# Gates by tanh on ScalarE and two products on VectorE in place of silu, in a cross-attention and FP4 feed-forward kernel

## The chip, the cores and the metric

The kernel runs on one core of a Trainium2 chip. The metric is the device time in microseconds (us) of one execution. PE is TensorE, DVE is VectorE, ACT is ScalarE, POOL is GpSimd, SP is the queue that issues the DMAs.

## What is computed

Two layers, each with a residual, on x of 4096 rows (2 x 2048) by 512. The first is an additive cross-attention over 77 tokens, which takes a tanh of every (row, token, channel), reduces it over the 512 channels to scores `rho`, and makes of a softmax over the tokens two gates for each row. The second is a feed-forward layer whose inputs are quantised to FP4 in blocks of 16:

```
h = jnp.tanh(txt_proj[:, None, :, :] + feat_proj[:, :, None, :] + b)   # (rows, 77, 512)
rho = jnp.einsum('bftd,d->bft', h, w[:, 0])
att = jax.nn.softmax(rho + (1.0 - qm)[:, None, :] * NEG, axis=-1)
w_s, b_s = tanh(txt_h . Wcw + bcw), tanh(txt_h . Wcb + bcb)
x = x + w_s * layernorm(x) + b_s
...
gate = fp4_linear(x, w_gate)       # 512 -> 1408
y = fp4_linear(x, w_up)
h = jax.nn.silu(gate) * y
x = x + fp4_linear(h, w_down)      # 1408 -> 512
```

## The kernel before

The scores are made in four blocks of 1024 rows. A block has 77 "quads": ACT writes tanh for four (token, channel group) pairs by 1024 rows into a slot of a ring (`tanh_quad`, L619, four instructions), and PE multiplies the slot by `w` and adds it into the score bank `rho` (`score_quad`, L797). For some quads DVE adds the token's bias first (`sum_quads`, L966, four instructions), and ACT takes all four parts in one instruction (L614). The ring has two slots in block 1 and three in blocks 2 and 3, so ACT can start a quad only when PE is through with the one that had its slot.

The feed-forward layer runs over 32 tiles of 128 rows. A tile has four column groups n = 0 to 3 of 352. For each, PE fills a gate bank and an up bank (`gate_up`, L875; two pairs of banks, `gu0` for even and `gu1` for odd n), ACT makes silu of the gate bank in `sg` (`silu_gate`, L652), and DVE multiplies it by the up bank into `hbuf` (`hidden`, L1270), which frees the pair of banks for group n + 2. Then `quantise_hidden` (L986 to L1022) makes FP4 values of the tile's 1408 columns, a DMA turns them, and PE runs `down` (L889).

The layers overlap: while tiles 0 to 6 run, block 1 is scored, with tiles 7 to 14 block 2, with tiles 15 to 22 block 3. The order of each engine's work is written out: PE runs a `gate_up` or a third of a `down` and then one to three quads; ACT runs some quads ahead of PE and then a silu; DVE runs each group's `hidden`, the next tile's `rows_tile`, `quantise_hidden` and the sums. Nearly every DVE instruction waits for the one before it (`step`, `signal`).

At the end of a block (tiles 6, 14 and 22, `SOFTMAX_AT`) a softmax goes round the engines: DVE drains `rho` (L1185), PE turns it, DVE subtracts the maxima (L1193), ACT takes exp (L627), DVE sums (L1212 to L1218) into `garg`, ACT takes tanh of that (`softmax_gates`, L646), and DVE, for the last block POOL, makes the rows' factors from it. `FREE_FROM` is 22. From tile 23 on no quads are left, and ACT has little to do.

A function of ACT needs its set of tables. Where the set changes the compiler puts in an ACT_TABLE_LOAD.

Of the kernel before, what the change touches and what calls it, by code (L numbers as in the profile page):

```python
# [7 lines left out]
ALU = mybir.AluOpType  # L8
ACT = mybir.ActivationFunctionType
# [20 lines left out]
PART = 640  # L30


def bass_xattn_fp4_ffn(nc, x, ctx_in, mask_in, Ws_in, W_in, w_in, b_in, Wcw_in, bcw_in, Wcb_in, bcb_in,
# [3 lines left out]
    INNER = gate_in.shape[0]  # L37
# [5 lines left out]
    NT = BATCH * SEQ // P  # L43
# [5 lines left out]
    GU_N = INNER // 4  # L49
# [35 lines left out]
    for k in range(1, NBLK):  # L85
# [5 lines left out]
        n = QPB - (PRE_QUADS if k == 1 else 0)  # L91
# [9 lines left out]
    n = QPB + PRE_QUADS  # L101
# [25 lines left out]
    with ctx:  # L127
        def sb(name, shape, dt=F32):
            return ctx.enter_context(nc.sbuf_tensor(name, shape, dt))

        def pb(name, cols):
            return ctx.enter_context(nc.psum_tensor(name, [P, cols], F32))

        def sem(name):
            return ctx.enter_context(nc.semaphore(name))
# [22 lines left out]
        hbuf = work[:, 0:INNER]  # L158
# [3 lines left out]
        hq = hq_flat.rearrange("p (h d) -> p h d", h=2)  # L162
# [11 lines left out]
        sg = sb("sg", [P, 2, GU_N])  # L174
# [41 lines left out]
        h_ordered = spare[:, 5 * D:5 * D + INNER]  # L216
# [3 lines left out]
        last_hq = [last_room[:, 2 * a:2 * b] for a, b in PARTS]  # L220
        h_size = featT[:, 0, 0:INNER]
# [4 lines left out]
        gu = [[pb(f"gu{i}{n}", 512) for n in "gu"] for i in range(2)]  # L226
# [73 lines left out]
        sg_ready = sem("sg_ready")  # L300
        gu_drained = [sem(f"gu_drained{i}") for i in range(2)]
# [7 lines left out]
        h_ordered_ready = sem("h_ordered_ready")  # L309
# [240 lines left out]
        def _(act):  # L550
# [91 lines left out]
            def softmax_gates(k):  # L642
                act.wait_ge(garg_ready, k + 1)
                n = BLOCKS[k] // P
                for u in range(2):
                    act.activation(gates[:, u, 0:n], garg[:, u, 0:n], ACT.Tanh,  # L646
                                   bias=bc[:, u:u + 1]).then_inc(gates_ready, 1)

            def silu_gate(t, n):

                act.wait_ge(gu_filled[n % 2], 2 * t + n // 2 + 1)
                act.activation(sg[:, n % 2, :], gu[n % 2][0][:, 0:GU_N], ACT.Silu,  # L652
                               scale=1.0 / W_PRE).then_inc(sg_ready, 1)

            def rows_last(t):

# [16 lines left out]
            def order_hidden(t, a, b, count):  # L673

                act.wait_ge(gu_drained[0], 2 * t + (1 if b == PART else 2))
                act.wait_ge(gu_drained[1], 2 * t + (1 if b <= 3 * GU_N else 2))
                act.activation(h_ordered[:, a:b].rearrange("p (i q b) -> p i q b", q=QB, b=BPC),
                               hbuf[:, a:b].rearrange("p (i b q) -> p i q b", q=QB, b=BPC),
                               ACT.Copy).then_inc(h_ordered_ready, 1)
                act.wait_ge(h_ordered_ready, count)  # L680
# [10 lines left out]
            for t in range(NT):  # L691
                for n in range(GU_T):
                    while issued < min(before[t, n] + DEPTH[min(before[t, n], QUADS - 1) // QPB], QUADS):
                        tanh_quad(issued)
                        issued += 1
                    if t - 1 in SOFTMAX_AT and n == 0:
                        softmax_gates(SOFTMAX_AT[t - 1])
                    silu_gate(t, n)
                    if t == FREE_FROM and n == 2:
                        last_drain()  # L700
                    if t == NT - 1 and n == 1:
                        order_hidden(t, 0, PART, t - FREE_FROM + 1)
                if t in SOFTMAX_AT:
                    if issued < QUADS:
# [4 lines left out]
                    else:  # L709
                        softmax_exp(SOFTMAX_AT[t])  # L710
                if t == NT - 1:
# [9 lines left out]
        def _(pe):  # L721
# [182 lines left out]
            for t in range(NT):  # L904
                for p in range(7):
# [4 lines left out]
                    elif t > 0:  # L910
                        down(t - 1, p - 4)
                    if t in SOFTMAX_AT and p == 3 and t < FREE_FROM:
                        softmax_transposes(SOFTMAX_AT[t], 0)
                    for n in slots.get((t, p), ()):
# [14 lines left out]
        def _(dve):  # L929
            done, scales = [0], [0]  # L930

            def step(ins):

                done[0] += 1
                ins.then_inc(dve_step, 1)
                dve.wait_ge(dve_step, done[0])

            def signal(ins, s, count):

                ins.then_inc(s, 1)  # L940
                dve.wait_ge(s, count)
# [8 lines left out]
            tt = dve.tensor_tensor  # L950
            stt = dve.scalar_tensor_tensor
# [313 lines left out]

            def hidden(t, n, sums=True):

                dve.wait_ge(sg_ready, GU_T * t + n + 1)
                h = hbuf[:, n * GU_N:n * GU_N + GU_N]
                signal(tt(h, sg[:, n % 2, :], gu[n % 2][1][:, 0:GU_N], ALU.mult), gu_drained[n % 2], 2 * t + n // 2 + 1)  # L1270
                if sums:
                    sum_quads(before[t, n])

            def quantise_hidden(t, between=None, midway=None):
                lift = W_PRE
                if t > 0:
                    dve.wait_ge(h_turned, 16 * t)
                straight, size = None, hbuf
                if t >= FREE_FROM:
                    straight, size = (h_ordered[:, 0:INNER], h_ordered_ready, t - FREE_FROM + 1), h_size  # L1280
                signal(quantise(hbuf, INNER, hq[:, 0, :], hq[:, 1, :], size, SCALE_MIN * lift, H_PRE / lift,
                                straight=straight, at=before[t, 4], between=between,
                                midway=midway), hq_ready, t + 1)
                sum_quads(before[t, 5])

            def quantise_split(t, first, midway):

                dve.wait_ge(h_turned, 16 * t)
                a, b = slice(0, PART), slice(PART, INNER)
                step(quantise(hbuf[:, a], PART, hq[:, 0, a], hq[:, 1, a], hbuf[:, a], SCALE_MIN * W_PRE, H_PRE / W_PRE,  # L1290
                              midway=last_tops))
                hidden(t, 3)
                signal(quantise(hbuf[:, b], INNER - PART, hq[:, 0, b], hq[:, 1, b], h_size[:, b], SCALE_MIN * W_PRE,
                                H_PRE / W_PRE, straight=(h_ordered[:, b], h_ordered_ready, 1), first=first,
                                midway=midway), hq_ready, t + 1)

            def quantise_part(i):
                lift = W_PRE
                a, b = PARTS[i]
                n = b - a  # L1300
                signal(quantise(hbuf[:, a:b], n, last_hq[i][:, 0:n], last_hq[i][:, n:2 * n], hbuf[:, a:b], SCALE_MIN * lift,
                                H_PRE / lift, straight=(h_ordered[:, a:b], h_ordered_ready, NT - FREE_FROM + i)),
                       hq_ready, NT + i)

            def result(t):
# [12 lines left out]
            for t in range(NT):  # L1318
                begun = SOFTMAX_AT.get(t)
                ending = SOFTMAX_AT.get(t - 1)  # L1320
                if t not in (FREE_FROM + 1, FREE_FROM + 2):
                    hidden(t, 0)
# [67 lines left out]
```

## Time and profile before

| | |
|---|---|
| median of 3 runs | 1549.76 us (1546.88 to 1550.38) |
| the profiled execution | 1548.83 us |
| its span | 1547.0 us |
| busy: PE, ACT, DVE, POOL | 1436.5, 1363.7, 1179.6, 253.1 us |
| TensorE clock granted, mean | 0.983 |

The span is from the first to the last instruction of the core. An engine's busy time is a sum over stages with different limits, so it doesn't tell which engine sets the time of a stage. PE's instruction ends are modelled, and matmuls overlap, so their starts are what to read.

### The profile page before, as it was taken

To read this page: it belongs to the slowest core of one execution; us is meant where nothing else is said; L and a number is where in the kernel's file an instruction comes from. 1 tells how busy PE (TensorE), PEld (TensorE's weight loads), DVE (VectorE), ACT (ScalarE), POOL (GpSimd) and SP (SyncE) were. 2 spreads that over 40 slices of the span, in tenths; PEclk is the share of its full clock that TensorE was granted. 3 is DMA by queue.
4 is the path that set the end of the run, shared out by engine and by line. 5 is a ranking of instruction groups with operands and counts; after the bars stand their busy time and mean duration, and the time that the engine had idled before them with its cause. 6 is when DMAs were issued, how large, how long until landed. Compare 5 with 4: busy or idle time off the path is not lost.

```text
span 1547.0 us, 24416 instructions
## 1 busy us (share of the span) xinstructions
PE 1436.5 (93%) x9752; PEld 648.6 (42%) x9752; DVE 1179.6 (76%) x1956; ACT 1363.7 (88%) x1269; POOL 253.1 (16%) x433
## 2 busy tenths in 40 slices
PE   6979899866989999999999999989999999999998
PEld 3434444411333333333444444434444444555554
DVE  6499999864486666759676766698877787898887
ACT  5999999999999999999999999999999999433321
POOL 1032222210011011101011111011111111312211
PEclk9999999988999999999999999999999999999999
DMA  4133333330011111102111111112111111123332
GB/s 145 41 72 82 82 83 82 82 68 29 12 26 40 27 40 40 34 16 45 40 40 40 40 27 40 40 30 50 40 40 40 40 40 40 40 59 73 79 69 61
DMA packets 181878, 77.91 MB, mean 50 GB/s; under 512 B 163947, under 2 KB 165995, under 8 KB 181765
## 3 DMA queue, kind: packets, MB, share of 16 engines
q1 hardware_dynamic: 180544, 75.00, 21.3%
q8 instruction: 76, 1.25, 0.3%
q10 hardware_dynamic: 1221, 1.36, 0.3%
q14 instruction: 37, 0.30, 0.1%
HBM read 27.85 MB, written 8.39 MB: 23 GB/s over the span
## 4 chain that ended last, share of the span: by engine, by line
PE 51%; ACT 23%; DVE 22%; issue 2%; DMA 1%; POOL 1%; SPq 0%; ACTq 0%; DVEq 0%; POOLq 0%
PE rho L797 19%; ACT hring L619 14%; PE dn L889 10%; PE gu0g L875 5%; PE gu1g L875 5%; PE gu1u L875 5%; PE gu0u L875 5%; ACT hring L614 4%; DVE work L1000 2%; DVE work L1018 2%; DVE work L1019 2%; DVE featT L966 2%; DVE sm L986 2%; ACT featT L614 1%; ACT featT L619 1%
## 5 line engine op out<-in xcount | busy, mean ns | idle before, releaser
L619 ACT ACTIVATE hring<-featT,bias 128x1024 f32<-128x1024 f32 x708 | 751.1, 1160 | 10.2 <-PE rho L797 10.2
L797 PE MATMUL rho<-hring,wslide 128*32 128x512 f32 x3776 | 461.2, 614 | 56.8 <-ACT hring L619 49.5
L619 ACT ACTIVATE featT<-featT,bias 128x1024 f32<-128x1024 f32 x232 | 249.5, 1182 | 1.2 <-PE rho L797 1.2
L797 PEld LDWEIGHTS rho<-hring,wslide 128*32 128x32 f32 x3776 | 106.2, 111 | 333.7 <-issue 197.6
L889 PE MATMUL dn<-wd_room,turned 128*128 128x512 f16 x1023 | 230.6, 379 | 0.4 <-DMA turned<-work 0.3
L485 POOL TENSOR_SCALAR split_t<-sm 128x88 f32<-128x88 f32 (+3 forms) x93 | 22.7, 245 | 1138.7 <-DVE sm L989 1138.6
L614 ACT ACTIVATE hring<-featT 128x4096 f32<-128x4096 f32 x57 | 208.1, 3651 | 0.6 <-DVE featT L966 0.6
L966 DVE TENSOR_SCALAR featT<-featT,bias 128x1024 f32<-128x1024 f32 x256 | 175.5, 750 | 10.0 <-ACT hring L614 6.3
L1270 DVE TENSOR_TENSOR work<-sg,gu1u 128x352 f32<-128x352 f32 x64 | 33.4, 521 | 166.6 <-ACT sg L652 165.7
L889 PEld LDWEIGHTS dn<-wd_room,turned 128*128 128x128 f16 x1023 | 96.5, 98 | 145.4 <-issue 36.0
L797 PE MATMUL rho<-featT,wslide 128*32 128x512 f32 x1056 | 126.3, 596 | 4.0 <-ACT featT L619 3.2
L875 PE MATMUL gu1g<-wg,turned 128*128 128x352 f16 x768 | 125.4, 313 | 4.3 <-DVE work L1270 4.3
L875 PE MATMUL gu0g<-wg,turned 128*128 128x352 f16 x768 | 125.5, 313 | 4.0 <-DVE work L1270 3.2
L875 PE MATMUL gu1u<-wu,turned 128*128 128x352 f16 x768 | 125.0, 313 | 0.0
L875 PE MATMUL gu0u<-wu,turned 128*128 128x352 f16 x768 | 125.0, 313 | 0.0
L488 POOL TENSOR_TENSOR s_lo<-sm,s_hi 128x88 f16<-128x88 f32 (+3 forms) x93 | 110.3, 1186 | 7.3
L875 PEld LDWEIGHTS gu0g<-wg,turned 128*128 128x128 f16 x768 | 71.3, 98 | 75.4 <-issue 27.7
L875 PEld LDWEIGHTS gu1g<-wg,turned 128*128 128x128 f16 x768 | 71.8, 98 | 72.7 <-issue 28.5
L875 PEld LDWEIGHTS gu0u<-wu,turned 128*128 128x128 f16 x768 | 75.1, 98 | 39.4
L875 PEld LDWEIGHTS gu1u<-wu,turned 128*128 128x128 f16 x768 | 75.2, 98 | 39.3
L652 ACT ACTIVATE sg<-gu1g 128x352 f32<-128x352 f32 x64 | 30.8, 481 | 60.6 <-PE gu1u L875 60.6
L652 ACT ACTIVATE sg<-gu0g 128x352 f32<-128x352 f32 x64 | 30.9, 483 | 52.9 <-PE gu0u L875 52.8
(207 smaller groups left out, 1573.3 us busy)
## 6 DMA issues: line engine op xcount, KB each, us to landing
xt<-in_x SPq DMA_DIRECT2D x32, 256.0 KB, 2.9
out<-xt SPq DMA_DIRECT2D x32, 256.0 KB, 2.3
work<-in_x SPq DMA_DIRECT2D x10, 512.0 KB, 3.9
xt<-in_x SPq DMA_DIRECT2D x6, 512.0 KB, 3.9
xt<-in_L_ffn_w_gate SPq DMA_DIRECT2D x11, 256.0 KB, 2.8
xt<-in_L_ffn_w_up SPq DMA_DIRECT2D x11, 256.0 KB, 2.7
work<-in_L_ffn_w_down SPq DMA_DIRECT2D x2, 704.0 KB, 4.4
xt<-in_L_ffn_w_down SPq DMA_DIRECT2D x2, 704.0 KB, 4.3
```

The source lines that it names most:

```text
L488: pool.tensor_tensor(s_lo[:, 0:nb], s, s_hi[:, 0:nb], ALU.subtract).then_inc(split_ready, 1)
L614: act.activation(slot[s], featT[:, :, r:r + rows], ACT.Tanh).then_inc(tanh_ready, GRP)
L619: act.activation(slot[s][:, g, :], featT[:, e, ROW0[k]:ROW0[k] + rows], ACT.Tanh, bias=bias[:, e, base + tok:base + tok + 1]).then_inc(tan ...
L652: act.activation(sg[:, n % 2, :], gu[n % 2][0][:, 0:GU_N], ACT.Silu, scale=1.0 / W_PRE).then_inc(sg_ready, 1)
L797: last = pe.matmul(rho[SLOTW * g:SLOTW * g + SLOTW, hf * 512:hf * 512 + 512], wslide[:, e, SLOTW - 1 - r:2 * SLOTW - 1 - r], slot[s][:, g, ...
L875: last = pe.matmul(ps[:, 0:GU_N], xqT[:, a, k, :], w[:, bb, k, n * GU_N:n * GU_N + GU_N], start=(k == 0 and i == 0), stop=(k == KC - 1 and ...
L889: last = pe.matmul(dn[:, :], hqT[:, a, c, :], wd[:, bb, c, :], start=(c == 0 and i == 0), stop=(c == NC - 1 and i == 2))
L966: dve.tensor_scalar(featT[:, g, to:to + BLOCKS[k]], featT[:, e, ROW0[k]:ROW0[k] + BLOCKS[k]], bias[:, e, tok:tok + 1], None, ALU.add).then ...
L986: step(dve.tensor_reduce(am, v, axis=AX_X, op=ALU.max, apply_absolute_value=True))
L1000: ins = tt(a.rearrange("p (i q b) -> p i b q", **natural), src.rearrange("p (i b q) -> p i b q", **natural), r.rearrange("p (i b) -> p i b ...
L1018: step(tt(a, a, m, ALU.add))
L1270: signal(tt(h, sg[:, n % 2, :], gu[n % 2][1][:, 0:GU_N], ALU.mult), gu_drained[n % 2], 2 * t + n // 2 + 1)
```

## The change

For tiles before `BY_TANH` = `FREE_FROM` + 1 = 23, the gate is no longer silu(g) times u. ACT makes tanh(g / 2), DVE makes (tanh + 1) times g in one scalar_tensor_tensor that reads the gate bank, and then multiplies by u. The result is silu(g) times u, up to a constant factor that `lift` takes out in the quantisation. From tile 23 on silu stays. Tanh and exp lie in one set of tables, silu and tanh in another one in common.

```
@@ constants
+    BY_TANH = FREE_FROM + 1
+
+    def lift(t):
+        return 2.0 * W_PRE * W_PRE if t < BY_TANH else W_PRE
@@ silu_gate
                 act.wait_ge(gu_filled[n % 2], 2 * t + n // 2 + 1)
-                act.activation(sg[:, n % 2, :], gu[n % 2][0][:, 0:GU_N], ACT.Silu,
-                               scale=1.0 / W_PRE).then_inc(sg_ready, 1)
+                if t < BY_TANH:
+                    act.activation(sg[:, n % 2, :], gu[n % 2][0][:, 0:GU_N], ACT.Tanh,
+                                   scale=0.5 / W_PRE).then_inc(sg_ready, 1)
+                else:
+                    act.activation(sg[:, n % 2, :], gu[n % 2][0][:, 0:GU_N], ACT.Silu,
+                                   scale=1.0 / W_PRE).then_inc(sg_ready, 1)
@@ hidden
                 dve.wait_ge(sg_ready, GU_T * t + n + 1)
-                h = hbuf[:, n * GU_N:n * GU_N + GU_N]
-                signal(tt(h, sg[:, n % 2, :], gu[n % 2][1][:, 0:GU_N], ALU.mult), gu_drained[n % 2], 2 * t + n // 2 + 1)
+                if t < BY_TANH:
+                    step(stt(h, sg[:, n % 2, :], 1.0, gu[n % 2][0][:, 0:GU_N], ALU.add, ALU.mult))
+                    signal(tt(h, h, gu[n % 2][1][:, 0:GU_N], ALU.mult), gu_drained[n % 2], 2 * t + n // 2 + 1)
+                else:
+                    signal(tt(h, sg[:, n % 2, :], gu[n % 2][1][:, 0:GU_N], ALU.mult), gu_drained[n % 2], 2 * t + n // 2 + 1)
@@ the quantisers of hbuf: W_PRE becomes lift(t) in two constants, no instruction changes
```

ACT's order at the end of block 2 (tile 14 and the first group of tile 15), before. `stage` is the softmax's room, `gates` its result, `sg` the gate of a group; `hring` and `featT` are slots of the ring.

```order
L619 ACTIVATE hring<-featT,bias 128x1024 x4
L627 ACT_TABLE_LOAD
L627 ACTIVATE stage<-stage 128x4x77 x2
L619 ACTIVATE featT<-featT,bias 128x1024 x4
L614 ACTIVATE hring<-featT 128x4096
L619 ACTIVATE hring<-featT,bias 128x1024 x4
L646 ACTIVATE gates<-garg,bc 128x8 x2
L652 ACT_TABLE_LOAD
L652 ACTIVATE sg<-gu0g 128x352
```

The same place of the changed kernel, whose lines are numbered four or five higher there:

```order
L623 ACTIVATE hring<-featT,bias 128x1024 x4
L631 ACTIVATE stage<-stage 128x4x77 x2
L623 ACTIVATE featT<-featT,bias 128x1024 x4
L618 ACTIVATE hring<-featT 128x4096
L623 ACTIVATE hring<-featT,bias 128x1024 x4
L650 ACTIVATE gates<-garg,bc 128x8 x2
L657 ACTIVATE sg<-gu0g 128x352
```

Two table loads are gone here, and nothing changes places. Over the whole program there were eight loads, ahead of the first copy, the first silu, each block's exp from block 1 on and the first silu after it; two stand in the changed kernel, the first and the one ahead of tile 23's silu.

DVE's order at the drain of block 2's scores (tile 14), before; `work` holds `hbuf`:

```order
L1185 TENSOR_SCALAR stage<-rho,negm 128x1024
L1270 TENSOR_TENSOR work<-sg,gu0u 128x352
L966 TENSOR_SCALAR featT<-featT,bias 128x1024 x4
L1192 TENSOR_REDUCE mx<-tr 128x4
L1193 TENSOR_TENSOR stage<-tr,mx 128x4x77
L1192 TENSOR_REDUCE mx<-tr 128x4
```

and in the changed kernel:

```order
L1193 TENSOR_SCALAR stage<-rho,negm 128x1024
L1279 SCALAR_TENSOR_TENSOR work<-sg,gu0g 128x352
L1280 TENSOR_TENSOR work<-work,gu0u 128x352
L974 TENSOR_SCALAR featT<-featT,bias 128x1024 x4
L1200 TENSOR_REDUCE mx<-tr 128x4
L1201 TENSOR_TENSOR stage<-tr,mx 128x4x77
L1200 TENSOR_REDUCE mx<-tr 128x4
```

One instruction more stands ahead of each product with the up bank, 92 in all (23 tiles of four groups), and everything behind it on DVE keeps its place.

## Rows read from the trace of the kernel before

**Rows 1.** Busy time by stage: start:end, length, busy us (instructions) of each engine.
```profile
core 0: us, PE busy (x) PEld busy (x) DVE busy (x) ACT busy (x) POOL busy (x), PEclk, DMA share, GB/s
395.00:693.00 298.00, 275.40 (x1983) 109.59 (x1982) 203.69 (x286) 296.05 (x249) 35.42 (x52) 1.00 0.14 29
693.00:1002.00 309.00, 303.13 (x2189) 127.67 (x2187) 223.67 (x323) 308.92 (x281) 42.64 (x60) 1.00 0.18 40
1002.00:1079.00 77.00, 71.65 (x511) 31.48 (x508) 71.58 (x122) 75.15 (x68) 11.10 (x16) 1.00 0.23 40
1080.00:1290.00 210.00, 209.99 (x1524) 89.80 (x1523) 161.00 (x225) 210.00 (x178) 29.77 (x44) 1.00 0.17 38
```

**Rows 2.** Groups of ACT's table loads: count, busy us, mean ns, idle before.
```profile
L652 ACT ACT_TABLE_LOAD x4 | 5.1, 1283 | 0.1
...
L627 ACT ACT_TABLE_LOAD x2 | 2.6, 1283 | 0.0
```

**Rows 3.** Timeline of ACT at 385 to 397: start, length, instructions merged.
```profile
384.72 10.49 ACT L619 ACTIVATE hring<-featT,bias 128x1024 f32<-128x1024 f32 x10
...
396.52 0.46 ACT L652 ACTIVATE sg<-gu0g 128x352 f32<-128x352 f32 x1
```

**Rows 4.** Groups of DVE's instructions, shapes kept apart.
```profile
L1270 DVE TENSOR_TENSOR work<-sg,gu1u 128x352 f32<-128x352 f32 x64 | 33.4, 521 | 166.6 <-ACT sg L652 165.7
...
L1309 DVE SCALAR_TENSOR_TENSOR xt<-dn,xt 128x512 f32<-128x512 f32 x31 | 21.4, 690 | 0.8
```

**Rows 5.** Timeline of DVE at 418 to 448, idle before and its releaser in brackets.
```profile
418.26 0.52 DVE L1270 TENSOR_TENSOR work<-sg,gu1u 128x352 f32<-128x352 f32 x1 [5.77 <-ACT sg L652]
...
437.05 0.52 DVE L1270 TENSOR_TENSOR work<-sg,gu0u 128x352 f32<-128x352 f32 x1
437.60 0.52 DVE L1270 TENSOR_TENSOR work<-sg,gu1u 128x352 f32<-128x352 f32 x1
...
445.29 2.74 DVE L966 TENSOR_SCALAR featT<-featT,bias 128x1024 f32<-128x1024 f32 x4
```

**Rows 6.** Timeline of ACT at 448.
```profile
448.14 3.62 ACT L614 ACTIVATE hring<-featT 128x4096 f32<-128x4096 f32 x1 [0.57 <-DVE featT L966]
```

**Rows 7.** Timeline of DVE at 678 to 719.
```profile
678.39 1.28 DVE L1185 TENSOR_SCALAR stage<-rho,negm 128x1024 f32<-128x1024 f32 x1 [9.16 <-PE rho L797]
...
718.84 0.52 DVE L1270 TENSOR_TENSOR work<-sg,gu1u 128x352 f32<-128x352 f32 x1 [0.30 <-ACT sg L652]
```

**Rows 8.** Timeline of PE at 720: tile 7's last gate.
```profile
719.73 1.95 PE L875 MATMUL gu1g<-wg,turned 128*128 128x352 f16 x12
```

**Rows 9.** Timeline of DVE at 1002 to 1085.
```profile
1002.45 1.28 DVE L1185 TENSOR_SCALAR stage<-rho,negm 128x1024 f32<-128x1024 f32 x1 [8.95 <-PE rho L797]
...
1040.86 0.52 DVE L1270 TENSOR_TENSOR work<-sg,gu0u 128x352 f32<-128x352 f32 x1
...
1078.30 0.52 DVE L1270 TENSOR_TENSOR work<-sg,gu0u 128x352 f32<-128x352 f32 x1
...
1084.93 0.52 DVE L1270 TENSOR_TENSOR work<-sg,gu1u 128x352 f32<-128x352 f32 x1 [6.11 <-ACT sg L652]
```

**Rows 10.** Timeline of PE at 1079: tile 16's third gate.
```profile
1078.87 1.96 PE L875 MATMUL gu0g<-wg,turned 128*128 128x352 f16 x12 [0.29 <-DVE work L1270]
```

**Rows 11.** Timeline of ACT at 1033: the gates of block 2.
```profile
1032.87 0.49 ACT L646 ACTIVATE gates<-garg,bc 128x8 f32<-128x8 f32 x2 [0.94 <-DVE garg L1218]
```

**Rows 12.** Timeline of DVE at 1273.
```profile
1273.10 0.51 DVE L1270 TENSOR_TENSOR work<-sg,gu0u 128x352 f32<-128x352 f32 x1
```

**Rows 13.** Timeline of PE at 1274 and 1311.
```profile
1274.35 1.95 PE L875 MATMUL gu0g<-wg,turned 128*128 128x352 f16 x12
...
1310.89 1.92 PE L797 MATMUL rho<-hring,wslide 128*32 128x512 f32 x16
```

**Rows 14.** Timeline of ACT at 1313: its last two quads.
```profile
1313.46 4.40 ACT L619 ACTIVATE hring<-featT,bias 128x1024 f32<-128x1024 f32 x4
```

**Rows 15.** Timeline of DVE at 1322 to 1332: tile 22's last two groups.
```profile
1322.47 0.52 DVE L1270 TENSOR_TENSOR work<-sg,gu0u 128x352 f32<-128x352 f32 x1 [0.80 <-ACT sg L652]
...
1331.37 0.52 DVE L1270 TENSOR_TENSOR work<-sg,gu1u 128x352 f32<-128x352 f32 x1
```

More of the change, by code:

```diff
@@ L1266, in hidden @@
             def hidden(t, n, sums=True):
+                h = hbuf[:, n * GU_N:n * GU_N + GU_N]
                 dve.wait_ge(sg_ready, GU_T * t + n + 1)
-                h = hbuf[:, n * GU_N:n * GU_N + GU_N]
-                signal(tt(h, sg[:, n % 2, :], gu[n % 2][1][:, 0:GU_N], ALU.mult), gu_drained[n % 2], 2 * t + n // 2 + 1)
+                if t < BY_TANH:
[3 more added lines that the diff above has]
+                    signal(tt(h, sg[:, n % 2, :], gu[n % 2][1][:, 0:GU_N], ALU.mult), gu_drained[n % 2], 2 * t + n // 2 + 1)
                 if sums:
@@ L1280, in quantise_hidden @@
                     straight, size = (h_ordered[:, 0:INNER], h_ordered_ready, t - FREE_FROM + 1), h_size
-                signal(quantise(hbuf, INNER, hq[:, 0, :], hq[:, 1, :], size, SCALE_MIN * lift, H_PRE / lift,
+                signal(quantise(hbuf, INNER, hq[:, 0, :], hq[:, 1, :], size, SCALE_MIN * lift(t), H_PRE / lift(t),
                                 straight=straight, at=before[t, 4], between=between,
@@ L1289, in quantise_split @@
                 a, b = slice(0, PART), slice(PART, INNER)
-                step(quantise(hbuf[:, a], PART, hq[:, 0, a], hq[:, 1, a], hbuf[:, a], SCALE_MIN * W_PRE, H_PRE / W_PRE,
+                step(quantise(hbuf[:, a], PART, hq[:, 0, a], hq[:, 1, a], hbuf[:, a], SCALE_MIN * lift(t), H_PRE / lift(t),
                               midway=last_tops))
                 hidden(t, 3)
-                signal(quantise(hbuf[:, b], INNER - PART, hq[:, 0, b], hq[:, 1, b], h_size[:, b], SCALE_MIN * W_PRE,
-                                H_PRE / W_PRE, straight=(h_ordered[:, b], h_ordered_ready, 1), first=first,
+                signal(quantise(hbuf[:, b], INNER - PART, hq[:, 0, b], hq[:, 1, b], h_size[:, b], SCALE_MIN * lift(t),
+                                H_PRE / lift(t), straight=(h_ordered[:, b], h_ordered_ready, 1), first=first,
                                 midway=midway), hq_ready, t + 1)
             def quantise_part(i):
-                lift = W_PRE
                 a, b = PARTS[i]
                 n = b - a
-                signal(quantise(hbuf[:, a:b], n, last_hq[i][:, 0:n], last_hq[i][:, n:2 * n], hbuf[:, a:b], SCALE_MIN * lift,
-                                H_PRE / lift, straight=(h_ordered[:, a:b], h_ordered_ready, NT - FREE_FROM + i)),
+                signal(quantise(hbuf[:, a:b], n, last_hq[i][:, 0:n], last_hq[i][:, n:2 * n], hbuf[:, a:b], SCALE_MIN * lift(NT - 1),
+                                H_PRE / lift(NT - 1), straight=(h_ordered[:, a:b], h_ordered_ready, NT - FREE_FROM + i)),
                        hq_ready, NT + i)
```

1 line of the change is left out of this document (removed).

## The prediction

> **What bounds the kernel now.** I read the stages first [rows 1]. From 395 to 1290 ACT is busy nearly all the time, 296.1 of 298 us, 308.9 of 309, 75.2 of 77 and 210.0 of 210, so at first sight whatever leaves ACT shortens the kernel. PE has idle time in the first stage (22.6 us) and the second (5.9), but none in the fourth: 209.99 of 210. There both engines are full, and a delay of PE that enters it comes out at its end. In the third stage, around the softmax of block 2, DVE is the busy one: 71.6 of 77 us.
>
> Then I went down DVE's timeline and looked for where it waits, since the change gives work to it. Over the whole run it waits some 167 us for the silus of odd groups alone [rows 4], but not everywhere. From 1002.45, where it drains the scores that PE has just ended, to 1084.93, where it waits for ACT again, there is no idle time on it but a wait for PE's transposes, which themselves wait for DVE [rows 9]. At the end of that run PE stands and waits for DVE's product: gate group 2 of tile 16 can start at 1078.87 only because the product that began at 1078.30 has ended [rows 9, 10]. The same shape stands at the end of block 1: DVE runs from 678.39 to 718.84 with 0.30 us of idle time that ACT ended, and the product that starts then ends at 719.36, 0.37 before PE's last gate of tile 7 needs its bank [rows 7, 8].
>
> **What the change removes.** By the two orders six loads go, not five: the first silu's, two each at the ends of blocks 1 and 2, and the last exp's. Each lasted 1.28 us [rows 2]. What a load costs its queue is read from starts: ten tanhs begin at 384.72 and last 10.49, so, at 1.04 from start to start, the next instruction would begin at 395.12; behind the load it begins at 396.52 [rows 3]. That is 1.40 a load. Five lie where ACT is full: 7.0 us. The sixth, at tile 22, is worth nothing, since DVE is busy with that tile's quantisation and has the exps before it asks for them.
>
> The Trainium skill ("ScalarE: Activation LUTs", What ACT_TABLE_LOAD costs) gives 2.66 us for a switch, 1.28 for the load and 1.38 for a drain. By it five loads would be 13.3 us. The trace shows the 1.28 and no drain behind it, and the sum goes by the 1.40.
>
> **What it adds.** Tanh in place of silu on the same 352 columns costs ACT the same, by the nearest rows: both are one pass at about one column a ns. DVE gets 92 scalar_tensor_tensors, half of whose operands lie in PSUM. The product beside it is of the same size, with one operand in PSUM: 0.52 [rows 4]; two such follow each other at 0.55 [rows 5]. The instruction of that very form in the trace is 512 wide and takes 0.69 [rows 4]. So a piece costs between 0.55 and 0.72 from start to start; I take 0.555, as the width is 352. In all 51 us, most of it under DVE's waits for ACT. What counts is how many stand in each run of DVE that has no idle time and whose end somebody waits for:
>
> (A) Block 1. DVE waits for ACT at 418.26; from there three pieces (tile 0 group 3, tile 1 groups 0 and 1) come before the sum that starts at 445.29 and ends 2.74 later, and ACT has already waited 0.57 us for it [rows 5, 6]. 3 x 0.555 = 1.7 us later, against 1.4 gained just before: ACT goes on at +0.3, the sign being that of a loss. Other sums of this block are in time by 0.6 or more behind a single piece, as I read them one by one, and cost nothing.
>
> (B) End of block 1, counted from PE's last score. Four pieces (tile 6 groups 2 and 3, tile 7 groups 0 and 1) stand between the drain and the end of the product at 718.84: 2.2, less the 0.30 of idle time and the 0.37 in hand, so PE's gate of group 3 starts 1.6 later [rows 7, 8]. ACT meanwhile has two loads less, 2.8, of which it waits away 0.9 for the softmax's sums. But a ring of three slots ties it to a PE that is 1.6 late, and most of its lead goes. PE has the stage's 5.9 us of idle time, nearly all waits for ACT, to win back what it lost [rows 1]. I put both at +0.2 when block 2's last score is done. With (A): +0.5.
>
> (C) End of block 2. Seven pieces stand in the run from 1002.45 to the end of the product at 1078.30: tile 14 groups 2 and 3, the four of tile 15, tile 16 group 0 [rows 9]. 7 x 0.555 = 3.9 us, and PE waits for its end already [rows 10]. The two loads that ACT loses here don't help: it waits for the softmax's sums as it is, 0.94 us [rows 11], which come 1.1 later now, and the products are held by DVE and not by silus. So PE enters the full stage at +4.4; I write +4.3 for what of ACT's gain DVE may use.
>
> (D) To the end of block 3. PE can't win it back [rows 1]. Around 1273 four pieces since DVE's last wait (2.2 us) meet 0.73 us in hand [rows 12, 13], by which PE falls back another 1.3 against ACT. ACT's second last quad starts at 1313.46, and the slot is that of the quad which PE ends about 1312.8, 1.9 after it started at 1310.89 [rows 13, 14]: 0.6 in hand. So ACT is dragged behind PE to +4.8.
>
> (E) Tile 22. ACT's last silu frees the product at 1322.47, behind 0.80 us of idle time that takes up what DVE is late by but 0.3; from there to the gates of the last softmax DVE runs without a stop, with that product and the one at 1331.37 on its way [rows 15]: 0.3 + 2 x 0.555 = +1.4.
>
> Behind tile 23 nothing is changed. Sum: 0.3 + 0.2 + 3.8 + 0.5 + 1.4 = +6.2 us. The profiled execution took 1548.83, 1.8 more than its span, and would take 1555.0; the median of the runs shown is 0.9 above it. I say 1555.5. About 0.2% (3 us) is what a measurement of this kernel can tell from no change.
>
> **The rivals.** (1) ACT's gain comes through, faster. This needs DVE's runs to have more room than I read: the gates at (C) would have to be released by ACT and not by DVE. Then 7.0 is gained, 1.4 is lost at (E), and the time is 1549.8 - 5.6 = 1544. The decision falls at 1078.87: from 3.9 us in hand there it holds, and the row shows a wait of 0.29 instead [rows 10]. For it speaks only that ACT is full in every stage [rows 1]. By the page's 2.66 a load the gain would be 6.3 us more, and the time 1538; what speaks against it is the row. Chance 0.13 for both.
>
> (2) Losses and gains nearly cancel: (A) and (C) are as written, but ACT keeps the 1.9 it leads by at (B), PE follows it over the stage's idle time, and 1 to 2 us of (D) and (E) stay hidden. That gives +1 to +3, about 1551.5. Chance 0.22.
>
> (3) The piece costs more than the product beside it, up to 0.72, being of a form with three operands that reads a bank beside that which PE fills. All costs, 3, 4, 7, 4 and 2 pieces, grow by 0.165 each, some 3.3 us, and the time is about 1559. Chance 0.10.
>
> My forecast, +6.2 by DVE's full runs, has 0.55.
>
> **How the numbers follow.** Slower by over 0.2% are my forecast and (3), 0.65 together. Of (2) most lies within 0.2%: 0.22. Faster is (1): 0.13. The range leaves out (1) and the top of (3): it starts at 1547.5, the low side of (2) less the spread of runs, and ends at 1559.5. The likeliest case alone: 1553 to 1558.
>
> **What would show it.** Two table loads on ACT; a busy time of DVE higher by 48 us and of ACT lower by 7.7. ACT waiting about 2 us for the sum at tile 1. PE's wait for a product at tile 16, now 0.29, grown to 2 us or more, and the tile 7 one new. ACT waiting for PE's quads in blocks 2 and 3, where it waits for almost nothing now; its wait for `garg` at tile 15 at 3 us. From tile 23 on the stretch to the end as long as before. The prediction is wrong if PE's gates at tiles 7 and 16 start no later behind the block's last score than before, or if the fourth stage has idle time on PE that takes up the delay.

## The result and the profile after

The changed kernel takes 1556.49 us, the median of 6 runs (1555.02 to 1559.39), against 1549.22 us before in 6 runs. The ratio is 1.0044, with a 95% interval of 1.0034 to 1.0054: slower by 5.3 to 8.4 us. The profiled execution spans 1553.2 us, 6.2 more than the one before.

The sums of the page move as the orders say. This is the busy line of the changed kernel; DVE has 47.4 us more, for 92 instructions more, and ACT 7.4 less. PE's share is unchanged.

```profile
PE 1439.0 (93%) x9752; PEld 650.4 (42%) x9752; DVE 1227.0 (79%) x2048; ACT 1356.3 (87%) x1263; POOL 252.3 (16%) x433
```

The groups of the changed kernel (line, engine, operation, count, busy us, mean ns, idle before) give the prices. The added operation takes 521 ns, like the product beside it, so the piece is 0.555 and not 0.72. Of eight loads two are left. A gate by tanh takes 453 ns.

```profile
L1279 DVE SCALAR_TENSOR_TENSOR work<-sg,gu1g 128x352 f32<-128x352 f32 x46 | 23.9, 521 | 129.8 <-ACT sg L657 129.2
L563 ACT ACT_TABLE_LOAD x1 | 1.3, 1283 | 2.4 <-issue 2.4
L660 ACT ACT_TABLE_LOAD x1 | 1.3, 1283 | 0.0
L657 ACT ACTIVATE sg<-gu1g 128x352 f32<-128x352 f32 x46 | 20.8, 453 | 4.3 <-PE gu1u L883 4.3
```

Now the places of the prediction, one after the other. DVE's timeline of the changed kernel at the end of block 2, which answers to [rows 9]:

```profile
1003.40 1.28 DVE L1193 TENSOR_SCALAR stage<-rho,negm 128x1024 f32<-128x1024 f32 x1 [8.13 <-PE rho L805]
...
1082.58 0.51 DVE L1279 SCALAR_TENSOR_TENSOR work<-sg,gu0g 128x352 f32<-128x352 f32 x1
1083.13 0.52 DVE L1280 TENSOR_TENSOR work<-work,gu0u 128x352 f32<-128x352 f32 x1
...
1087.63 0.52 DVE L1279 SCALAR_TENSOR_TENSOR work<-sg,gu1g 128x352 f32<-128x352 f32 x1 [3.98 <-ACT sg L657]
```

And PE's, at tile 7's last gate, tile 16's third and tile 21's third, which answer to [rows 8, 10, 13]:

```profile
722.07 1.96 PE L883 MATMUL gu1g<-wg,turned 128*128 128x352 f16 x12 [1.19 <-DVE work L1280]
...
1083.71 1.96 PE L883 MATMUL gu0g<-wg,turned 128*128 128x352 f16 x12 [1.66 <-DVE work L1280]
...
1280.44 1.96 PE L883 MATMUL gu0g<-wg,turned 128*128 128x352 f16 x12 [1.10 <-DVE work L1280]
```

From the drain to the product that PE waits for DVE has no idle time but its wait for the transposes, as before. From the drain's start to the start of tile 16's third gate it was 1078.87 - 1002.45 = 76.42 us, and it is 1083.71 - 1003.40 = 80.31 now: 3.89 more, seven pieces of 0.555. The three gates start 2.3, 4.8 and 6.1 us later than before, each behind a wait for DVE that has grown or is new; at tile 16 it is 1.66 us, where the prediction named 2 or more.

Stages of the changed kernel (start:end, length, busy us of PE, PEld, DVE, ACT, POOL; granted clock), the fourth moved with the work:

```profile
1003.00:1084.00 81.00, 74.96 (x512) 32.69 (x509) 75.22 (x129) 74.64 (x68) 11.13 (x16) 0.96 0.19 38
1084.00:1297.00 213.00, 211.90 (x1535) 90.71 (x1533) 173.91 (x249) 211.18 (x179) 29.84 (x44) 1.00 0.19 38
```

The fourth stage has 1.1 us of idle time on PE, which is its wait at 1280 and no room to win anything back.

One thing stands there that wasn't forecast: a granted clock of 0.96 in the third stage, where before it was 1.00. Four stretches of 3.4 us at the lower of TensorE's two levels, 1.2 GHz, come up at 437, 686, 1011 and 1045, where the kernel before has none between 386 and its end.

### The profile page after: what moved, and what is told of

Its sections match the earlier page's. It is cut to its first block, busy times and chain, and to the rows that moved or that the text cites. A ratio compares the mean times of both kernels' runs of the same rounds, so it can differ in the third digit from the quotient of the medians.

```text
span 1553.2 us, 24502 instructions
## 1 busy us (share of the span) xinstructions
PE 1439.0 (93%) x9752; PEld 650.4 (42%) x9752; DVE 1227.0 (79%) x2048; ACT 1356.3 (87%) x1263; POOL 252.3 (16%) x433
## 3 DMA queue, kind: packets, MB, share of 16 engines
q8 instruction: 76, 1.25, 0.3%
## 4 chain that ended last, share of the span: by engine, by line
PE 50%; DVE 27%; ACT 18%; issue 2%; DMA 1%; POOL 1%; SPq 0%; DVEq 0%; ACTq 0%; POOLq 0%
PE rho L805 18%; ACT hring L623 12%; PE dn L897 10%; PE gu0g L883 5%; PE gu0u L883 5%; PE gu1g L883 5%; PE gu1u L883 4%; ACT hring L618 4%; DVE work L1008 3%; DVE featT L974 2%; DVE work L1026 2%; DVE work L1027 2%; DVE sm L994 2%; DVE sm L998 1%; DVE work L1023 1%
## 5 line engine op out<-in xcount | busy, mean ns | idle before, releaser
L623 ACT ACTIVATE hring<-featT,bias 128x1024 f32<-128x1024 f32 x708 | 748.1, 1140 | 13.3 <-PE rho L805 13.1
L897 PE MATMUL dn<-wd_room,turned 128*128 128x512 f16 x1023 | 233.9, 383 | 0.5 <-DMA turned<-work 0.5
L1279 DVE SCALAR_TENSOR_TENSOR work<-sg,gu1g 128x352 f32<-128x352 f32 x46 | 23.9, 521 | 129.8 <-ACT sg L657 129.2
L1008 DVE TENSOR_TENSOR work<-work,sm 128x1408 f32<-128x1408 f32 (+1 forms) x25 | 72.5, 2900 | 0.9
L491 POOL TENSOR_TENSOR s_hi<-split_t,split_d 128x88 f16<-128x88 f32 (+3 forms) x93 | 63.5, 683 | 7.3
```

Of the source, the lines that this page charges most:

```text
L491: small(pool.tensor_tensor(s_hi[:, 0:nb], t, d, ALU.subtract))
L623: act.activation(slot[s][:, g, :], featT[:, e, ROW0[k]:ROW0[k] + rows], ACT.Tanh, bias=bias[:, e, base + tok:base + tok + 1]).then_inc(tan ...
L897: last = pe.matmul(dn[:, :], hqT[:, a, c, :], wd[:, bb, c, :], start=(c == 0 and i == 0), stop=(c == NC - 1 and i == 2))
L1008: ins = tt(a.rearrange("p (i q b) -> p i b q", **natural), src.rearrange("p (i b q) -> p i b q", **natural), r.rearrange("p (i b) -> p i b ...
```

## Experiments

All ran in 5 rounds beside the kernel before. The times of one kernel lie 2 to 3 us to either side of their median, much of it from before the first gate: in three profiles whose programs are the same up to there PE starts it at 388.80 (before), 388.92 (changed) and 393.56 (`loads_only`). So beside the ratios I give a distance within one trace, from the drain of block 2 to tile 16's third gate, which doesn't contain that.

A second distance runs from tile 0's third gate to the end of the span. It leaves out the start as well, and with it the first silu's load. These are PE's rows around that gate before, and the gate's row in the changed kernel:

```profile
401.18 1.92 PE L797 MATMUL rho<-hring,wslide 128*32 128x512 f32 x16 [1.23 <-ACT hring L619]
403.04 1.96 PE L875 MATMUL gu0g<-wg,turned 128*128 128x352 f16 x12
...
401.74 1.97 PE L883 MATMUL gu0g<-wg,turned 128*128 128x352 f16 x12
```

From there to the end it is 1547.0 - 403.04 = 1144.0 us before and 1553.2 - 401.74 = 1151.5 in the changed kernel, 7.5 more. From the first gate to the third it is 14.24 us before and 12.82 in the changed kernel, a load's worth less. But it is 12.80 in `pieces_only` and in `before_fewer_sums` too, which keep that load: there PE's quad ahead of the first gate took 3.6 us at the lower clock, and not 1.9, and PE does not wait for ACT afterwards. So what the first load costs depends on where an execution's ACT stands, between nothing and 1.4 us. Each of these distances is from one execution.

### The loads alone, and the products alone

`loads_only` is the changed kernel without the added operation: tanh's gate is multiplied by the up bank alone, so the output isn't silu's.

```
                 if t < BY_TANH:
-                    step(stt(h, sg[:, n % 2, :], 1.0, gu[n % 2][0][:, 0:GU_N], ALU.add, ALU.mult))
-                    signal(tt(h, h, gu[n % 2][1][:, 0:GU_N], ALU.mult), gu_drained[n % 2], 2 * t + n // 2 + 1)
+                    signal(tt(h, sg[:, n % 2, :], gu[n % 2][1][:, 0:GU_N], ALU.mult), gu_drained[n % 2], 2 * t + n // 2 + 1)
```

Expected:

> The changed kernel without the added product of VectorE: the gates are tanh times the up bank, so the output is not silu's; six table loads are gone and nothing is added. Theory (VectorE's runs without idle time decide): only the three loads ahead of block 2's end come through, since behind it the run from the drain to tile 16 holds TensorE as before and TensorE is full afterwards: 3 x 1.4 = 4.2 us less, about 1545.0. Rival (ScalarE is the bound wherever it is full): five loads, 7.0 us less, 1542.2.

Measured: 1546.68 against 1550.43, ratio 0.9977 (0.9966 to 0.9988), 3.6 us less. The two rows that make the distance, of `loads_only`, PE's first and then DVE's:

```profile
1079.63 1.96 PE L883 MATMUL gu0g<-wg,turned 128*128 128x352 f16 x12 [0.31 <-DVE work L1279]
...
1003.24 1.28 DVE L1193 TENSOR_SCALAR stage<-rho,negm 128x1024 f32<-128x1024 f32 x1 [8.95 <-PE rho L805]
```

76.39 us, and 76.42 before: the two loads that ACT loses between these rows bring nothing. That is the theory's half, the gain is that of three loads within its interval (1.9 to 5.3); the rival's 7.0 is outside. From tile 0's third gate to the end it is 1547.4 - 406.51 = 1140.9 us, 3.1 less than before, where the two loads behind that gate and ahead of block 2's drain are 2.8.

`pieces_only` keeps silu and all loads, and adds the operation with a result that is overwritten, so it computes what the reference asks.

```
-                signal(tt(h, sg[:, n % 2, :], gu[n % 2][1][:, 0:GU_N], ALU.mult), gu_drained[n % 2], 2 * t + n // 2 + 1)
+                if t < BY_TANH:
+                    step(stt(h, sg[:, n % 2, :], 1.0, gu[n % 2][0][:, 0:GU_N], ALU.add, ALU.mult))
+                signal(tt(h, sg[:, n % 2, :], gu[n % 2][1][:, 0:GU_N], ALU.mult), gu_drained[n % 2], 2 * t + n // 2 + 1)
```

Expected:

> Silu and all eight loads stay, and the added product of VectorE is made too, its result overwritten: the cost of the 92 products alone. Theory: by the same places as in the prediction, without the gain of the loads: 2.1 at tile 1, 0.2 at tile 7, 3.9 at tiles 14 to 16, 0.5 and 1.4 at the end, 8.1 us more than before, 1557.3, within 1 us of the changed kernel. Rival (gains and losses simply add, so the products cost what the change lost and what the loads gave back, 7.3 + 4.2 to 7.3 + 7.0): 1561 to 1563.5.

Measured: 1560.33, ratio 1.0061 (1.0049 to 1.0074), 9.5 us more (7.6 to 11.5). The 8.1 is in the interval, and the rival's 11.5 to 14 begins just at its upper end. But the median is 3.8 us above the changed kernel's, where I expected 1: the gain of the loads is not used up as far as I thought. 9.5 lost and 3.6 won would make 5.9, and the change measures 6.8, so within the intervals the two do add, if the gain is taken as measured and not as five loads. The traces say the same: from tile 0's third gate to the end `pieces_only` has 1555.3 - 401.35 = 1154.0 us, 10.0 more than before, and 10.0 - 3.1 = 6.9 against the changed kernel's 7.5. The part that I had too small lies ahead of block 2's drain, which comes 1005.55 - 401.35 = 604.2 us behind that gate, and 599.4 before: 4.8 later, where I had 2.3. It is 4.2 later at tile 7's last gate (722.23 - 401.35 against 719.73 - 403.04) and didn't win that back.

### Seven products out of 92

`without_run` leaves out the seven pieces of the run behind block 2's drain, `run_alone` makes those seven alone. Where a piece is left out the gate is tanh times the up bank.

```
+    RUN = {(14, 2), (14, 3), (15, 0), (15, 1), (15, 2), (15, 3), (16, 0)}
...
-                    step(stt(h, sg[:, n % 2, :], 1.0, gu[n % 2][0][:, 0:GU_N], ALU.add, ALU.mult))
-                    signal(tt(h, h, gu[n % 2][1][:, 0:GU_N], ALU.mult), gu_drained[n % 2], 2 * t + n // 2 + 1)
+                    if (t, n) not in RUN:
+                        step(stt(h, sg[:, n % 2, :], 1.0, gu[n % 2][0][:, 0:GU_N], ALU.add, ALU.mult))
+                    signal(tt(h, h if (t, n) not in RUN else sg[:, n % 2, :], gu[n % 2][1][:, 0:GU_N], ALU.mult), gu_drained[n % 2],
+                           2 * t + n // 2 + 1)
```

(`run_alone` has `in` for `not in`.) Expected of `without_run`:

> The changed kernel with 85 of the 92 added products: the seven of tile 14 groups 2 and 3, tile 15, and tile 16 group 0 are left out (their gate is tanh times the up bank). Theory: this run alone carries 3.9 us, 1552.6. Rival (the cost is spread evenly over 92 products): 7/92 of the loss of 7.3 to 12 us, under 1 us, 1555.6. Rival (the windows at half TensorE clock are the cost): the four of them took up to 1.7 us each; if those at 1011 and 1045 vanish with the seven products, 3.4 us less; if they stay, nothing.

and of `run_alone`:

> The changed kernel with seven of the 92 added products, those of tile 14 groups 2 and 3, tile 15, and tile 16 group 0; the others are left out. Theory: 3.9 us more than with none of them, about 1549, so that seven products of 0.55 us use up all that the loads gave. Rival (cost spread evenly): under 1 us more than with none.

Measured: `without_run` 1554.78, ratio 1.0026 (1.0018 to 1.0035), against 1.0044 with all: 2.8 us less. `run_alone` 1551.0, ratio 1.0007 (0.9997 to 1.0018), against 0.9977 with none: 4.6 us more. The intervals of such differences are some 2 us wide on either side, and they hold 3.9 both times. The distance is sharper: 1082.35 - 1005.99 = 76.36 in `without_run` and 80.34 in `run_alone`. Spread evenly over the 92, the 10.4 us between all and none would be 0.8 for the seven. The low stretch at 1045 went with the seven pieces and the one at 1011 too, so by times alone the clock would be a rival still. The distance says that it isn't one: `run_alone` has neither of them and keeps the 3.9. Its only one lies in tile 16's gate itself, behind the end of the distance, and it does cost time: the gate takes 3.4 us and not 1.8, and from its start to the end of the span it is 1551.4 - 1081.95 = 469.5 us, against 1547.4 - 1079.63 = 467.8 in `loads_only`, where likewise no added product stands behind it. PE has no idle time in that stage. So of the 4.6 us some 1.7 can be the clock's.

### Where the products stand

The sharpest cut: 20 pieces stand in runs without idle time whose end somebody waits for, by the timeline of before; 72 don't. `in_runs_20` makes the first, `in_waits_72` the second, by the same edit with this set.

```
+    RUNS = {(0, 3), (1, 0), (1, 1), (6, 2), (6, 3), (7, 0), (7, 1), (14, 2), (14, 3), (15, 0), (15, 1), (15, 2), (15, 3),
+            (16, 0), (20, 1), (20, 2), (20, 3), (21, 0), (22, 2), (22, 3)}
```

Expected of the 72:

> The changed kernel with 72 of the 92 added products, those that by the timeline of before follow a wait of VectorE for ScalarE and have time in hand behind them; the other 20 (tile 0 group 3 to tile 1 group 1, tile 6 group 2 to tile 7 group 1, tile 14 group 2 to tile 16 group 0, tile 20 group 1 to tile 21 group 0, tile 22 groups 2 and 3) are left out, so their gate is tanh times the up bank. Theory: the 72 cost nothing, though they are 40 us of VectorE's time: the ratio of the kernel with none, 0.998, about 1546.5 to 1547. Rival (each product costs something): the kernel with all loses 6.8 + 3.6 = 10.4 us against the one with none, 72/92 of it is 8 us: 1554.5.

and of the 20:

> The complement: the changed kernel with those 20 added products alone. Theory: 11 us of VectorE's time that carry all of the loss: as the changed kernel, 1556 to 1557. Rival (each product costs something): 20/92 of 10.4 us above the kernel with none, 1549.

Measured:

| kernel | added products | DVE time of them | ratio to before | us against before | tile 0's third gate to the end, against before |
|---|---|---|---|---|---|
| `loads_only` | 0 | 0 | 0.9977 (0.9966 to 0.9988) | -3.6 | -3.1 |
| `in_waits_72` | 72 | 40 | 0.9988 (0.9979 to 0.9996) | -1.9 | -1.8 |
| `in_runs_20` | 20 | 11 | 1.0031 (1.0019 to 1.0043) | +4.8 | +6.8 |
| changed kernel | 92 | 51 | 1.0044 (1.0034 to 1.0054) | +6.8 | +7.5 |

Twenty pieces cost 8.4 us, 72 cost 1.7, together 10.1, and all cost 10.4. By the last column it is 9.9, 1.3 and 10.6. So the place decides: 0.42 us a piece in the runs, and 0.024 in the waits. The 1.7 isn't clear of zero (the intervals overlap), but a part of it is in the traces: one of the 72 stands ahead of a sum that ACT comes for at 910, and ACT waits for it, 0.58 us in the changed kernel, 0.62 in `in_waits_72`, and not at all in `loads_only` and `in_runs_20`. I had left that place out. The changed kernel's row:

```profile
910.18 3.62 ACT L618 ACTIVATE hring<-featT 128x4096 f32<-128x4096 f32 x1 [0.58 <-DVE featT L974]
```

These are the rows of `in_runs_20`, PE's and DVE's:

```profile
1082.30 1.96 PE L885 MATMUL gu0g<-wg,turned 128*128 128x352 f16 x12 [2.02 <-DVE work L1283]
...
1001.99 1.28 DVE L1195 TENSOR_SCALAR stage<-rho,negm 128x1024 f32<-128x1024 f32 x1 [8.95 <-PE rho L807]
```

80.31 us from DVE's drain to PE's gate, as in the changed kernel. In `in_waits_72` it is 76.43, as before.

### What the stretches at the lower clock cost

`group_in_gap` moves one product of the changed kernel, at tiles 6 and 14, from ahead of the softmax's first shift into the gap in which DVE waits for the second transposes.

```
                     softmax_drain(begun)
-                    hidden(t, 2)
+                    sum_quads(before[t, 2])
                     softmax_shift(begun, 0)
+                    hidden(t, 2)
                     softmax_shift(begun, 1)
```

(The sum is made by `hidden` otherwise; the added call keeps it ahead of the first shift.) Expected:

> The changed kernel with one move on VectorE, at tiles 6 and 14: the product of group 2 stands between the two shifts of the softmax, where VectorE waits 1.3 us for TensorE's second transposes, and no longer ahead of the first. The transposes wait for VectorE 0.55 us less, 1.27 again. Theory of the runs without idle time: each of the two runs is 0.6 us shorter, the first is won back anyway, so 0.6 us less than the changed kernel, 1555.9 of 1556.5. Rival (the two windows at half TensorE clock behind the transposes cost time): if they go with the longer wait, up to 1.7 us each, together 2 to 3 us less, 1553.5 to 1554.5. If the windows go and the time stays, they stood on no path.

Measured: 1558.28 (1553.37 to 1558.57), ratio 1.0045 (1.0031 to 1.0058), the changed kernel's within the intervals. PE at block 1's transposes and the `down` behind them, in the changed kernel:

```profile
685.30 1.09 PE L870 MATMUL tr<-gat,stage 128*128 128x77 f32 x8 [1.82 <-DVE stage L1201]
686.23 4.44 PE L897 MATMUL dn<-wd_room,turned 128*128 128x512 f16 x12
```

and in `group_in_gap`:

```profile
686.18 1.09 PE L870 MATMUL tr<-gat,stage 128*128 128x77 f32 x8 [1.18 <-DVE stage L1201]
687.10 2.75 PE L897 MATMUL dn<-wd_room,turned 128*128 128x512 f16 x12
```

PE waits 1.82 us for the shift in the one and 1.18 in the other, and behind the longer wait the same twelve matmuls take 4.44 us and not 2.75. The low stretch at 1011 goes in the same way. The time doesn't: DVE's run decides when PE goes on. The run got shorter as expected, 1083.98 - 1004.30 = 79.68 against 80.31, and 0.6 us is less than the medians can show. From tile 0's third gate to the end `group_in_gap` has 1553.5 - 403.26 = 1150.2 us, 1.2 less than the changed kernel. Two runs of DVE shortened by 0.6 are that 1.2, which leaves nothing for these two stretches, nor for the one at 1045, which is gone too. They stood on no path, and the one in `run_alone` above stood on one: what such a stretch costs depends on where it falls.

### Handing sums back to ACT

If DVE's runs are too long, and ACT has time to give, quads whose bias DVE adds can go back to ACT: 2.7 us less for DVE each, 0.65 more for ACT. `before_fewer_sums` and `after_fewer_sums` do it for five of them, `rebalanced` for seven.

```
-    SUMS = {1: range(12, QPB, 3), 2: [3, *range(11, QPB, 4)], 3: [2, 5, *range(11, QPB, 3)]}
+    SUMS = {1: [q for q in range(12, QPB, 3) if q != 21], 2: range(11, QPB, 4),
+            3: [q for q in range(11, QPB, 3) if q != 68]}
```

(`rebalanced`: block 2 as it was, `range(20, QPB, 3)` in block 3.) Expected of `before_fewer_sums`:

> Silu and the loads as before, but five quads are no longer added up by VectorE first (block 1's 22nd, block 2's fourth, block 3's third, sixth and 69th): each takes 2.7 us from one of VectorE's full runs and gives ScalarE 0.65. A control for the next kernel. Theory: the run behind block 2's drain is 5.4 us shorter, but ScalarE has 2 us more to do by then and no loads less, so TensorE waits for ScalarE where it waited for VectorE: within 1.5 us of before, 1548.5 to 1551. Rival (VectorE's run alone holds the kernel): 3 to 5 us less, 1545.

of `after_fewer_sums`:

> The changed kernel with the same five quads left to ScalarE, which has time since its loads went. Theory: at tile 1 -1.3 instead of +0.3, at tile 7 -2.1, at tiles 14 to 16 -1.4 instead of +3.9, at tile 21 0, at tile 22 +1.4: 3.4 us less than before, 1546 against 1549.4, and 10 less than the changed kernel. Rival (the added products cost the same wherever they stand): within 2 us of the changed kernel, 1555 to 1558.

of both edits on the changed kernel, `after_fewer_sums_gap`:

> Both edits on the changed kernel. Theory: the runs of VectorE no longer hold TensorE, so the move adds nothing: within 1 us of the kernel with five sums less. If TensorE's wait at its transposes brings a slow window there, and the move takes it away, 1 to 2 us less.

and of `rebalanced`:

> The changed kernel with seven quads left to ScalarE: block 1's 22nd, the first five that VectorE summed in block 3, and the 69th there; block 2's fourth is summed again, since taking it away only made VectorE wait for TensorE. Theory, after the kernel with five sums less (1555.0, ratio 1.0034): the run at tiles 14 to 16 loses another 8 us and no longer holds TensorE, but ScalarE has 2 us more to do there, so 0.5 to 1.5 us less than that kernel, ratio 1.0025 to 1.003. Rival (it all hangs on VectorE's run): the 0.8 us that TensorE still fell back there and the 2.1 it could lead by are gained, ratio 1.0015.

Measured: `before_fewer_sums` 1551.02, ratio 1.0002 (0.9993 to 1.0011), no change, as expected. `after_fewer_sums` 1555.0, ratio 1.0034 (1.0021 to 1.0047): some 1.6 us under the changed kernel, within the intervals, and not the 10 that I expected. In the traces it is 4.2 (1552.0 - 404.75 = 1147.3 from tile 0's third gate to the end), still less than half. The rival's 1555 to 1558 fits the median as well; that added products cost the same wherever they stand is what the table above excludes. `after_fewer_sums_gap` 1554.53, ratio 1.0027 (1.0017 to 1.0036), the same within its interval. `rebalanced` 1556.14, ratio 1.0034 (1.0022 to 1.0046), no better: the theory's 1.0025 to 1.003 is in the interval, and the rival's 1.0015 isn't. None of them beats the kernel before.

What made the expectation of `after_fewer_sums` too high shows in its DVE timeline. At the end of block 1 the time that the sum left turned into idle time:

```profile
681.20 1.28 DVE L1194 TENSOR_SCALAR stage<-rho,negm 128x1024 f32<-128x1024 f32 x1 [8.60 <-PE rho L806]
...
685.71 0.48 DVE L1201 TENSOR_REDUCE mx<-tr 128x4 f32<-128x308 f32 x1 [2.11 <-PE tr L871]
```

The sum had stood between the product and the reduction, and DVE now waits 2.11 us there for PE's transposes. So what such a sum was worth was its length less that wait. At the end of block 2 DVE waits the same 2.11 us for the transposes, and the distance is 1082.13 - 1004.95 = 77.18, 3.1 us less than in the changed kernel where two sums are 5.3. In `rebalanced`, with three more of them gone, it is 75.00, with DVE waiting for ACT:

```profile
1083.17 0.52 DVE L1280 SCALAR_TENSOR_TENSOR work<-sg,gu0g 128x352 f32<-128x352 f32 x1 [5.43 <-ACT sg L658]
```

There the run is no longer the bound, and ACT is. It has 0.65 us more to do for each quad that came back. That `rebalanced` is no faster than `after_fewer_sums`, although this distance is 2.2 us shorter, the times alone don't settle, with intervals 2 us wide on either side. The traces show where it is lost: block 2's drain comes 602.8 us behind tile 0's third gate in `rebalanced` and 600.2 in `after_fewer_sums`. Of these 2.6 us 1.5 are there at tile 1 already, whose third gate ran at the lower clock. From its start to that of the next it is 451.40 - 442.59 = 8.81 us, against 7.26 in `after_fewer_sums`:

```profile
442.59 3.52 PE L884 MATMUL gu0g<-wg,turned 128*128 128x352 f16 x12 [2.23 <-DVE work L1281]
```

How the rest divides between the sum that block 2 makes again and another stretch at the lower clock at 691 stays open.

## Why the prediction was right, and where it wasn't

The forecast was 1555.5 and slower; 1556.49 was measured, and of the profiled executions +6.2 us was forecast and found. The mechanism of its largest term, DVE's run behind block 2's drain, is shown; some of the smaller terms came out by errors that cancel. By its steps:

| step | forecast, us behind before | trace |
|---|---|---|
| (A) behind tile 1, ACT | +0.3 | 448.89 - 448.14 = +0.75 |
| (B) tile 7's last gate, PE, without (A) | +1.6 | 722.07 - 719.73 - 0.75 = +1.6 |
| (B) drain of block 2 | +0.5 | 1003.40 - 1002.45 = +0.95 |
| (C) the run behind it | +3.9 | +3.89 |
| (C) tile 16's third gate, PE | +4.3 | 1083.71 - 1078.87 = +4.84 |
| (D) tile 21's third gate, PE | +5.6 | 1280.44 - 1274.35 = +6.09 |
| (D) ACT's second last quad | +4.8 | 1318.69 - 1313.46 = +5.2 |
| (E) from there to the last block's gates | +1.4 | +1.1 |

Rows of ACT in the changed kernel for the first and the last two:

```profile
444.72 4.27 ACT L623 ACTIVATE hring<-featT,bias 128x1024 f32<-128x1024 f32 x4 [1.42 <-PE rho L805]
448.89 3.60 ACT L618 ACTIVATE hring<-featT 128x4096 f32<-128x4096 f32 x1
...
1318.69 4.27 ACT L623 ACTIVATE hring<-featT,bias 128x1024 f32<-128x1024 f32 x4
...
1345.64 0.49 ACT L650 ACTIVATE gates<-garg,bc 128x8 f32<-128x8 f32 x2 [5.81 <-DVE garg L1226]
```

(C), the largest term, is shown by four kernels: with the seven pieces the distance is 80.3, whatever else is in, and without them 76.4. That the loads behind it bring nothing is shown by `loads_only`. That what PE loses there isn't won back is in the fourth stage's row.

(A) came out at +0.75 and not +0.3. I had ACT wait for a sum of DVE. In the changed kernel's trace ACT doesn't wait for that sum at all, it waits 1.42 us for PE's quads before it. PE had stood 2.21 us for DVE's first product of tile 1, and from the start of the gate behind that to the next bank's it was 3.4 us and not 1.8, as its clock was at the lower level. PE's row of the changed kernel:

```profile
437.46 3.54 PE L883 MATMUL gu0g<-wg,turned 128*128 128x352 f16 x12 [2.21 <-DVE work L1280]
```

So the sum came in time only because the ring was late already. Where the clock stayed up, the forecast's wait is there: ACT waits 1.15 us for the sum in `pieces_only` and 1.13 in `without_run`, whose program up to here is the changed kernel's.

```profile
451.46 3.62 ACT L619 ACTIVATE hring<-featT 128x4096 f32<-128x4096 f32 x1 [1.13 <-DVE featT L975]
```

Counted from tile 0's third gate this instruction starts at 45.1 us before, 46.8 in `without_run` and 47.2 in the changed kernel. So three pieces cost the 1.7 us of the forecast, and the stretch at the lower clock 0.3 more. Whether the 0.3 reaches the end isn't shown: from the third gate to the end the changed kernel has 3.8 us more than `without_run`, which the seven products alone explain. The 1.4 that the forecast sets against the 1.7 is the first load's, which not every execution pays for.

(B) is right for tile 7 (1.6 us), and its +0.2 at the drain came out partly by luck. ACT doesn't wait for the softmax's sums at the end of block 1, where I had 0.9; its gates start at 709.34 without a wait. And PE had won back nearly all of (A) and (B) by 900: a gate that starts at 899.95 before starts at 900.07. Then the wait at 910 came in, which the forecast lacks. Without it, in `in_runs_20`, block 2's drain comes 600.9 us behind tile 0's third gate, and 601.7 in the changed kernel.

At (D) I took 1.3 us for PE, where my own terms, 2.2 less 0.73, give 1.5; the trace has 1.25. At (E) I had counted 0.3 us for a DVE that is late when ACT's silu comes; it was late by nothing, and two pieces make the 1.1. With such errors on either side the exact 6.2 is partly luck.

Of the signs that I named, ACT's wait for the sum at tile 1 did not come in the changed kernel, PE's wait at tile 16 is 1.66 us and not 2 or more, and ACT's wait for the softmax's sums at tile 15 is 1.23 us where I said 3: a quad ahead of it had already waited 3.39 for PE, as this part of ACT's timeline in the changed kernel shows.

```profile
1016.90 4.27 ACT L623 ACTIVATE hring<-featT,bias 128x1024 f32<-128x1024 f32 x4 [3.39 <-PE rho L805]
...
1034.93 0.49 ACT L650 ACTIVATE gates<-garg,bc 128x8 f32<-128x8 f32 x2 [1.23 <-DVE garg L1226]
```

Rival (1), ACT's gain coming through, is excluded by `loads_only`: even with nothing added the gain is 3.6 us, and 7.0 is outside its interval. The estimate of 13.3 us for five loads, from the 2.66 us a switch that the Trainium skill gives ("ScalarE: Activation LUTs", What ACT_TABLE_LOAD costs), finds no support either. At the end of block 1 tile 7's first silu starts 709.61 - 707.82 = 1.79 us behind the softmax's gates with a load between them, and 709.72 - 709.34 = 0.38 in the changed kernel without one: 1.41 for a load, as in the prediction, and no room for a drain of 1.38 beside it. Rival (2), the near balance, needed a part of (D) and (E) to stay hidden, and both are there in the trace, 6.09 at tile 21's gate and 1.1. Rival (3), a dearer piece, fell with its 521 ns.

## What to carry to other kernels

An engine that is idle a quarter of the time can still have stretches with no idle time at all, and work that is moved to it costs little outside them and its full length inside. Find them before moving: go from each wait of the engine to the next, count the new instructions between, and ask who waits for the end. Here 20 of 92 placed instructions carried 8.4 of 10.4 us.

A saving on a busy engine counts only up to the next point where another engine sets the pace; five loads of 1.40 us brought 3.6, because two of them stood where the softmax went round through the other engine, and the first is not on every execution's path. And what a removed instruction is worth on a full run must be read with the waits beside it: a sum of 2.7 us that stood ahead of a wait left 2.1 us of new waiting.

## What the runs showed of the hardware that was not expected

TensorE's clock fell to 1.2 GHz for 3.4 us behind waits that had grown only little. In the changed kernel it fell behind 1.82 us at both blocks' transposes, and behind 2.21 us at tile 1; behind 1.27 at the transposes and 1.15 at tile 1 (before), and 1.18 at the transposes (`group_in_gap`), it stayed at 2.4 GHz. The same twelve matmuls took 4.4 and 2.7 us. But the length of a wait alone doesn't tell. At tile 1 the gate is slow behind 2.21 us in the changed kernel and at full clock behind 2.22 in `without_run`. At block 2's transposes `in_runs_20` waits the same 1.82 us as the changed kernel, and its matmuls aren't slow:

```profile
1008.20 1.09 PE L872 MATMUL tr<-gat,stage 128*128 128x77 f32 x8 [1.82 <-DVE stage L1203]
1009.12 2.75 PE L899 MATMUL dn<-wd_room,turned 128*128 128x512 f16 x12
```

And in `in_runs_20` PE stands 2.02 us at tile 16 and its gate then takes no longer, while in `run_alone` the same gate behind 2.03 us took this long:

```profile
1081.95 3.40 PE L884 MATMUL gu0g<-wg,turned 128*128 128x352 f16 x12 [2.03 <-DVE work L1282]
```

What tells these apart stays open. What a stretch costs goes by its place: 1.7 us to the end of the program at tile 16 in `run_alone`, where PE has no idle time, nothing at block 1's and block 2's transposes, and at tile 1 0.3 us in the changed kernel and 1.5 in `rebalanced`. In `rebalanced` the sum that ACT would wait for behind that gate is gone, so PE's delay isn't hidden there.

Up to the first gate, where the changed kernel's program is that of before, the profiled executions differ by nearly 5 us (388.80 before, 393.56 in `loads_only`), with a granted clock of 0.94 and 0.92 over the first 395 us. Differences under some 5 us between single spans of this kernel say nothing of a change; distances inside a trace repeated to 0.1.
